# Two early expert tiles put among the last sequence's work, in products of 256 columns

## The chip, the cores and the metric

The kernel runs on one core of a Trainium2 chip. The time is device time of one execution in microseconds: the median of three runs before the change is 913.55 us (912.6 to 915.59). The engines are TensorE (PE; its weight loads are the row PEld), VectorE (DVE), ScalarE (ACT), GpSimd (POOL) and the DMA queue of SyncE (SP).

## What is computed

Two blocks on x of 16 sequences of 128 tokens and 256 columns, with a context of the same shape:

```
x = x + xattn0(layernorm(x), ctx)        # K K^T, lower triangle, times Q
x = x + ffn0(layernorm(x))               # RMS norm, 16-head causal attention of width 128 with rope,
                                         # then 2 of 8 experts per token: silu(t w1) * (t w3) w2, F 512
x = x + xattn1(layernorm(x), ctx)        # 16 heads of 64, softmax, output times tanh(gate)
x = x + ffn1(layernorm(x))               # 2 of 16 experts, F 256, and one shared expert
```

Each token goes to its two experts alone: the tokens are sorted into one run of rows per expert, and the experts work on tiles of 128 rows.

## The kernel before, in words

**Stages.** Sequence stage (b = 0 to 15): attention of both kinds, then for each sequence the router (`ra`, `cnt`, `rb`: places of its tokens in the experts' runs, L1740 to L1783), the cast of the places (`pi`) and a scatter of the token rows to memory (`sc`, two indirect DMAs, POOL). Expert stage 0: NT0 = 37 listed tiles beside the two early ones; the first 16 of the list are tiles of pairs with split weights (three products each, L829 to L831), the rest are single tiles (L1023). Then the cross attention with the gathers `ga` of the experts' results (L2328), expert stage 1, and the shared expert with the final sum.

**Early tiles.** AHEAD = 2 tiles are full whatever the last sequences hold. `a_route` (DVE, L1875 to L1910) lists them from the counts of COUNTED = 10 sequences; `a_xs` loads their rows (SP, L2398); then `a_xT` (two transposes, L1214), `a_xT_e` (ACT), `a_gate0/1`, `a_up0/1` (one product of 512 columns each, L1224, with the token rows as stationary operand; each is two records in the trace, as the type is f32), `a_silu` (ACT, L1480), `a_hm` (DVE, L1915), `a_hT` (L1234), `a_hT_e` (ACT, L1488), `a_down0/1` (two products of 256 columns each, L1243) and `a_y`. All take PSUM banks of the ring `s` (0 to 3), which the scores of the sequences use, so `a_xT` follows `s` of sequence 15.

**After sequence 15.** `route` (DVE, L1785 to L1873) makes the list of all expert tiles from the full counts and ends with two casts into TI (L1869, L1871). Behind it: `xs` loads the rows of a tile (SP, L2448), `wa`/`wv` (ACT L1395, DVE L2084) and `wdh`/`wdl` (ACT L1408, DVE L2053) split the expert's weights, `xT` transposes (L995), `xTh`/`xTl` (ACT L1417, DVE L2043) split the rows, and `gate` of tile 0 is the first expert product. `places` (DVE, L1917 to L1966, 27 instructions) lists where each token's results lie; the gathers `ga` wait for it and for the last store `ys` of results. `load_q` (L2500 on) loads the weights wq and wo of the cross attention (1 MB each), on SP, behind the last `down`.

**Order of the work.** No order is written by hand. `Plan.order` is a list scheduler: each phase has an engine, a booked duration in ns, what it follows, its banks and a due. Of all phases whose predecessors are laid out it takes the one with the smallest start + due, where due is that of the phase plus its LEAD from a table; it knows no table load of ACT and no clock. Each engine's instructions are issued in that order, so a phase that waits holds back those behind it on its engine. Sequence b has due 20 b; the early tiles have AHEAD_DUE = 400, and 20 more for the second.

**Names in the steps.** L932 and L923 scores, L1342 exp, L947 transposes of probabilities and L1349 their copies (the last two before PV are those of groups 2 and 0), L962 PV, L971 up-projection, L1731 residual, L1355 square, L979 and L980 count.

## Time and profile before

| | |
|---|---|
| median of 3 runs | 913.55 us |
| the profiled execution, its own time | 913.28 us |
| its span, first to last instruction | 911.5 us |
| mean granted TensorE clock | 0.985 |
| PE, DVE, ACT, POOL busy | 853.1, 709.4, 604.6, 287.2 us |

The stages by the trace: sequences to about 203 us, expert stage 0 from 214 to 403, cross attention from there to about 700, the rest to the end. Busy times are sums over the span; which engine sets the time differs by stage. The clock is given as a share of TensorE's full rate (1.00 is 2.4 GHz, 0.50 is 1.2 GHz; what lies between is a mean over a window).

### The profile page before, as it was taken

What the parts mean: (1) busy time and instruction counts of PE and PEld (TensorE: products, weight loads), DVE (VectorE), ACT (ScalarE), POOL (GpSimd) and SP (SyncE); (2) the same over time, 40 slices, a digit from 0 to 9 for tenths busy, and PEclk for the clock granted to TensorE, in tenths of its full rate; (3) what the DMA queues carried; (4) which work ended last, traced back from release to release, by engine and by line L of the source; (5) the groups of instructions that cost most, each with busy time, mean ns of one, the idle gap of its engine ahead of it and who ended that gap; (6) DMA issues with size and microseconds to landing.
All of it is one profiled execution on the core that took longest, in us unless ns stands there. A gap on an engine that the chain in (4) does not pass through costs nothing.

```text
span 911.5 us, 23338 instructions
## 1 busy us (share of the span) xinstructions
PE 853.1 (94%) x7726; PEld 762.7 (84%) x7726; DVE 709.4 (78%) x1990; ACT 604.6 (66%) x1718; POOL 287.2 (32%) x359
## 2 busy tenths in 40 slices
PE   5799989879999999996899999999999999999997
PEld 3677656538999999995898988998889889999996
DVE  4887898776887777786899888777688638888867
ACT  4388899956666676664777667778775327777740
POOL 3865577660000000005554542111023004444420
PEclk9999999979999999997999999999999999999999
DMA  8237700023312311031111121031044933333335
GB/s 316 74 117 269 320 24 26 31 87 112 116 59 70 141 47 59 25 109 50 34 42 36 43 81 67 19 100 36 2 185 191 366 76 92 103 94 100 101 113 200
DMA packets 43319, 94.23 MB, mean 103 GB/s; under 512 B 6112, under 2 KB 29536, under 8 KB 41664
## 3 DMA queue, kind: packets, MB, share of 16 engines
q1 hardware_dynamic: 36336, 73.93, 23.4%
q0 software_dynamic: 6864, 18.80, 6.0%
q8 instruction: 64, 1.05, 0.5%
q14 instruction: 55, 0.45, 0.2%
HBM read 63.53 MB, written 29.17 MB: 102 GB/s over the span
## 4 chain that ended last, share of the span: by engine, by line
PE 65%; DVE 8%; issue 2%; ACT 2%; DMA 1%; POOL 0%; ACTq 0%; SPq 0%; DVEq 0%; POOLq 0%
PE ps L1023 17%; PE ps L829 11%; PE ps L830 10%; PE ps L831 10%; PE ps L1116 3%; PE ps L1140 3%; PE ps L1126 3%; PE ps L1198 2%; DVE BIGR L2084 1%; PE ps L1224 1%; PE ps L995 1%; PE ps L996 1%; DMA ys_dram<-BIG 1%; DVE X L2119 1%; ACT BIGR L1395 1%
## 5 line engine op out<-in xcount | busy, mean ns | idle before, releaser
L829 PE MATMUL ps<-BIGR 128*128 128x256 f32 (+1 forms) x946 | 292.0, 309 | 7.5 <-DVE BIGR L2084 3.1
L831 PE MATMUL ps<-BIGR 128*128 128x256 f32 (+1 forms) x898 | 255.8, 285 | 0.0
L830 PE MATMUL ps<-BIGR 128*128 128x256 f32 (+1 forms) x722 | 211.7, 293 | 0.0
L829 PEld LDWEIGHTS ps<-BIGR 128*128 128x128 f32 x946 | 180.7, 191 | 14.3 <-issue 9.8
L1023 PE MATMUL ps<-BIG 128*128 128x128 f32 x1424 | 177.3, 275 | 0.0
L831 PEld LDWEIGHTS ps<-BIGR 128*128 128x128 f32 x898 | 171.1, 191 | 0.7
L1023 PEld LDWEIGHTS ps<-BIG 128*128 128x128 f32 x1424 | 168.1, 192 | 0.1
L830 PEld LDWEIGHTS ps<-BIGR 128*128 128x128 f32 x722 | 138.5, 192 | 1.8
L2328 POOL DMA_INDIRECT BIG<-ys_dram,YI x32 | 35.3, 1102 | 218.2 <-DMA ys_dram<-BIG 210.5
L1565 ACT ACTIVATE BIG<-ps,BIG 128x128 f32<-128x128 f32 x256 | 91.0, 383 | 13.2 <-DVE BIG L2164 12.9
L2313 POOL DMA_INDIRECT xs_dram<-TT,PI x64 | 65.5, 1023 | 86.2 <-ACT PI L1375 72.3
L2336 POOL DMA_INDIRECT yt_dram<-BIG,IX x47 | 55.3, 1177 | 115.4 <-DVE BIG L2077 112.8
L2053 DVE TENSOR_TENSOR BIGR<-BIG,BIGR 128x512 fp32r<-128x512 f32 (+1 forms) x76 | 67.9, 895 | 11.9 <-ACT BIGR L1408 9.2
L1342 ACT ACTIVATE BIG<-ps,BIG 128x128 f32<-128x128 f32 x256 | 71.7, 408 | 3.9 <-DVE BIG L1701 3.9
L830 PE MATMUL ps<-CTR,BIGR 128*128 128x256 f32 x224 | 63.2, 282 | 0.0
L2251 POOL TENSOR_TENSOR st<-st,CS 128x1 f32<-128x1 f32 (+1 forms) x48 | 30.4, 637 | 99.9 <-DVE st L1656 99.7
L2084 DVE TENSOR_TENSOR BIGR<-BIG,BIGR 128x1024 fp32r<-128x1024 f32 (+3 forms) x57 | 48.2, 864 | 15.8 <-ACT BIGR L1395 12.1
L1408 ACT CAST BIGR<-BIG 128x512 fp32r (+1 forms) x76 | 59.0, 777 | 0.0
L1565 ACT ACTIVATION_READ_ACCUMULATOR BIG<-ps,BIG 128x1 f32 x256 | 56.9, 222 | 0.0
L1573 ACT COPY BIG<-ps 128x512 f32<-128x512 f32 x64 | 38.6, 603 | 27.5 <-PE ps L1126 25.6
L2060 DVE TENSOR_TENSOR BIG<-ps,BIG 128x256 f32<-128x256 f32 (+1 forms) x84 | 45.2, 539 | 13.2 <-PE ps L1023 11.3
L1398 ACT COPY BIG<-BIG 128x512 f32 x47 | 29.1, 619 | 33.9 <-PE ps L1023 32.3
(304 smaller groups left out, 1873.4 us busy)
## 6 DMA issues: line engine op xcount, KB each, us to landing
BIG<-in_wgu SPq DMA_DIRECT2D x2, 6144.0 KB, 19.1
BIG<-in_wd SPq DMA_DIRECT2D x2, 4096.0 KB, 22.5
BIG<-xs_dram SPq DMA_DIRECT2D x47, 129.5 KB, 2.1
BIG<-xs_dram SPq DMA_DIRECT2D x37, 128.0 KB, 2.0
ys_dram<-BIG SPq DMA_DIRECT2D x37, 128.0 KB, 2.0
BIG<-in_wkv SPq DMA_DIRECT2D x2, 2048.0 KB, 9.5
kv_dram<-BIG SPq DMA_DIRECT2D x16, 256.0 KB, 2.1
BIG<-in_wgu SPq DMA_DIRECT2D x2, 2048.0 KB, 9.8
```

The lines of the kernel that those rows point to most:

```text
L829: pe.matmul(o, l[0], r[0], start=start, stop=False)
L830: pe.matmul(o, l[0], r[1], start=False, stop=False)
L831: return pe.matmul(o, l[1], r[0], start=False, stop=stop)
L1023: i = pe.matmul(o[:, c * 128:(c + 1) * 128], wt[:, at:at + 128], x[:, k * 128:(k + 1) * 128], start=k == 0, stop=k == 1)
L1342: i = act.activation(p_[g][:, at], ps("s", b, i=g)[:, at], ACT.Exp, bias=sm[:, 4 * g + n:4 * g + n + 1])
L1408: act.copy(D_[j % len(D_)][:, 0:n], WD[:, bass.ds(e * n, n)]).then_inc(S["down_hi"], 1)
L1565: i = act.activation(xp_[s % 4][:, at], ps("S", s // 2, i=s % 2)[:, at], ACT.Exp, bias=sm[:, 4 + n:5 + n], accum_out=sm[:, 8 + n:9 + n])
L2053: v.tensor_tensor(wd[:, n:2 * n], WD[:, bass.ds(e * n, n)], wd[:, 0:n].bitcast(F32), ALU.subtract).then_inc(S["down_lo"], 1)
L2060: v.tensor_tensor(h, ps("up", r_, j)[:, 0:F], h, ALU.mult).then_inc(*frees("up", r_, j))
L2084: return v.tensor_tensor(dst, src, hi.bitcast(F32), ALU.subtract)
L2313: pool.indirect_dma_start(XS if r else XS0, bass.IndirectOffsetOnAxis(ap=PI[:, b, k:k + 1], axis=0), TT[tile_of(r, b)][:, 0:ROW if r else ...
L2336: pool.indirect_dma_start(YT, bass.IndirectOffsetOnAxis(ap=IX[:, j:j + 1], axis=0), Y_[1][j % 3], None).then_inc(sem(f"results_placed{j % ...
```

## The change

- COUNTED is 9 instead of 10. The row loads of the early tiles wait for `ctx` of sequence 11 (COUNTED + 2) instead of 9.
- The first early tile has due 500 and takes banks of the ring `misc` (4 to 7), after `qkT` of sequence 15; the second has due 900 + 20 and the ring `s`, after `s` of sequence 15, as before. `a_route` has due 600.
- Gate, up and down of an early tile are four phases each of one product of 256 columns (booked 430 ns), where they were two of 860.
- `a_route` is four phases of 650 ns, `places` eight of 800 to 1250 ns, piece i after `wv` of tile 18 + i, due -2000 (it was one of 4400 after `wv` of tile 8, due 4000).
- `gate` of tile 0 follows `a_up3` of the second early tile, `gate` of tile 2 its `a_down3`.
- The table LEAD is replaced for the phases after the sequences; the leads of the sequence phases are the same, those of the early tiles are 0. Among the new ones: xTh0 533 to 1314, wa0 -172 to 643, xs0 -352 to -11820, load_q -19372 to -33060, ys0 -48558 to -13864, kwl -7379 to -26302, owl -17804 to -6563, gates_a -34755 to -23246.

```diff
-COUNTED = 10
-AHEAD_DUE = 400
+COUNTED = 9
+AHEAD_DUE = (500, 900)
+A_DUE = 600
...
-    p.add("DVE", 4400, ("places",), ("wv", 0, 8), due=4000)
+    for i, ns in enumerate((800, 950, 950, 950, 1250, 950, 950, 1250)):
+        p.add("DVE", ns, ("places", i), ("wv", 0, PAIRED + 2 + i), due=-2000)
...
-    p.add("DVE", 2200, ("a_route",), ("rb", 0, COUNTED - 1), due=AHEAD_DUE)
+    for i in range(4):
+        p.add("DVE", 650, ("a_route", i), ("rb", 0, COUNTED - 1), due=A_DUE)
...
-            p.add(engine, ns, (name, i), *after, banks=[("s", (q, i)) for q in banks], due=AHEAD_DUE + 20 * i, **kw)
-        add("SP", 700, "a_xs", ("a_route",), ("sc", 0, COUNTED - 1), ("ctx", COUNTED - 1), ("load_w0b",), late=2200)
-        add("PE", 220, "a_xT", ("a_xs", i), ("s", NB - 1), banks=["a_xT_e"])
-        add("PE", 860, "a_gate0", ("a_xT_e", i), ("a_reg", i), banks=["a_silu"])
-        add("PE", 860, "a_gate1", ("a_gate0", i))
-        add("PE", 860, "a_up0", ("a_gate1", i), banks=["a_hm"])
-        add("PE", 860, "a_up1", ("a_up0", i))
+            p.add(engine, ns, (name, i), *after, banks=[("s" if i else "misc", (q, i)) for q in banks], due=AHEAD_DUE[i] + 20 * i, **kw)
+        add("SP", 700, "a_xs", ("a_route", 3), ("sc", 0, COUNTED - 1), ("ctx", COUNTED + 2), ("load_w0b",), late=2200)
+        add("PE", 220, "a_xT", ("a_xs", i), ("s" if i else "qkT", NB - 1), banks=["a_xT_e"])
+        for which, bank in (("gate", "a_silu"), ("up", "a_hm")):
+            for x in range(4):
+                before = (f"a_{which}{x - 1}", i) if x else ("a_gate3", i) if which == "up" else ("a_xT_e", i)
+                add("PE", 430, f"a_{which}{x}", before, ("a_reg", i), banks=[] if x else [bank])
...
-            p.add("PE", 1440, ("gate", r, j), ("xTl", r, j0), ("wv", r, j), ("xTl", r, j0 + 1), banks=[("gate0", ("silu", r, j))], due=3 * j)
+            p.add("PE", 1440, ("gate", r, j), ("xTl", r, j0), ("wv", r, j), ("xTl", r, j0 + 1),
+                  *[("a_up3", AHEAD - 1) for _ in range(j == 0)], *[("a_down3", AHEAD - 1) for _ in range(j == 2)], banks=[("gate0", ("silu", r, j))], due=3 * j)
...
-                at = k * 2 * F0 + (F0 if which == "up" else 0)
-                m = pe.matmul(ps(*key)[:, :], AXT[i % 2][:, k * 128:k * 128 + 128],
-                              WGU[:, bass.ds(expert[i] * (4 * F0) + at, F0)], start=k == 0, stop=k == 1)
+                at = k * 2 * F0 + (F0 if which == "up" else 0) + half * D
+                m = pe.matmul(ps(*key)[:, half * D:half * D + D], AXT[i % 2][:, k * 128:k * 128 + 128],
+                              WGU[:, bass.ds(expert[i] * (4 * F0) + at, D)], start=k == 0, stop=k == 1)
```

## Rows read from the trace of the kernel before

**Rows 1.** Windows: us, PE, PEld, DVE, ACT, POOL busy (x instructions), PEclk, DMA share, GB/s

```profile
176.00:180.00 4.00, 3.21 (x47) 2.04 (x49) 2.75 (x13) 4.00 (x14) 1.19 (x2) 1.00 0.00 0
...
188.00:192.00 4.00, 2.36 (x36) 1.94 (x36) 1.40 (x11) 2.32 (x7) 2.64 (x4) 0.58 0.34 112
...
200.00:204.00 4.00, 4.00 (x8) 1.75 (x7) 3.51 (x23) 0.60 (x1) 1.96 (x3) 0.71 0.28 98
```

**Rows 2.** Chain of waits into the expert stage: start us, us, what

```profile
196.62 9.95 PE ps L1224 x16
...
213.03 1.05 DVE BIGR L2043 x4
...
214.32 0.35 PE ps L829
```

**Rows 3.** Timeline of DVE, last sequences: start us, us, engine, line, op, out<-in

```profile
184.43 0.15 DVE L1880 TENSOR_TENSOR sc<-CNT,CS 128x8 f32<-128x8 f32 x1
...
187.35 0.49 DVE L1731 SCALAR_TENSOR_TENSOR BIG<-BIG,st,ps 128x264 f32<-128x264 f32 x1
...
203.06 0.15 DVE L1871 CAST TI<-sc 128x1 int32<-128x1 f32 x1
```

**Rows 4.** Timeline of PE, last sequences and second early tile

```profile
180.24 1.08 PE L962 MATMUL ps<-BIG 128*32 128x128 f32 x32
...
184.10 0.67 PE L971 MATMUL ps<-small,BIG 128*128 128x264 f32 x2
...
189.84 1.94 PE L962 MATMUL ps<-BIG 128*32 128x128 f32 x32 [0.78 <-ACT BIG L1349]
...
193.53 1.22 PE L971 MATMUL ps<-small,BIG 128*128 128x264 f32 x2 [1.13 <-DVE BIG L1722]
...
202.97 3.60 PE L1224 MATMUL ps<-BIG,small 128*128 x8
```

**Rows 5.** Timeline of ACT over the same stretch

```profile
187.88 0.42 ACT L1355 ACTIVATE BIG<-BIG 128x256 f32<-128x256 f32 x1 [0.96 <-DVE BIG L1731]
...
198.57 1.28 ACT L1480 ACT_TABLE_LOAD   x1
200.43 0.60 ACT L1480 ACTIVATE CT<-ps 128x512 f32<-128x512 f32 x1 [0.57 <-PE ps L1224]
...
211.54 1.15 ACT L1417 ACTIVATE BIGR<-ps,small 128x128 fp32r<-128x128 f32 x4
```

**Rows 6.** Timeline of SP's queue: the first row loads of the expert stage

```profile
204.23 2.97 SPq L2448 DMA_DIRECT2D BIG<-xs_dram  x3
```

**Rows 7.** Page, DMA issues: out<-in, engine, xcount, KB each, us to landing

```profile
BIG<-xs_dram SPq DMA_DIRECT2D x37, 128.0 KB, 2.0
```

**Rows 8.** Timeline of PE in the expert stage: a pair tile and a single tile

```profile
250.55 0.33 PE L995 MATMUL ps<-CS,BIG 128*128 128x128 f32 x1
...
333.60 0.36 PE L829 MATMUL ps<-BIGR 128*128 128x256 f32 x1
```

**Rows 9.** Timeline of DVE in a single tile of the expert stage

```profile
331.08 0.69 DVE L2069 TENSOR_TENSOR BIGR<-BIG,BIGR 128x512 fp32r<-128x512 f32 x1 [0.56 <-ACT BIGR L1442]
332.15 1.23 DVE L2053 TENSOR_TENSOR BIGR<-BIG,BIGR 128x1024 fp32r<-128x1024 f32 x1 [0.38 <-ACT BIGR L1408]
```

**Rows 10.** Windows of the second boundary (columns as in the first group)

```profile
430.00:432.00 2.00, 2.00 (x15) 2.00 (x15) 1.96 (x3) 0.60 (x1) 2.00 (x1) 0.74 0.21 66
```

**Rows 11.** Timeline of PE at the second boundary

```profile
427.70 0.55 PE L829 MATMUL ps<-BIGR 128*128 128x256 f32 x1 [1.81 <-DVE BIGR L2084]
```

**Rows 12.** Timeline of DVE: places, first and last of its 27 instructions

```profile
403.84 0.16 DVE L1923 TENSOR_SCALAR BIG<-BIG 128x9 f32<-128x9 f32 x1
...
411.25 0.18 DVE L1966 CAST YI<-Y 128x32 int32<-128x32 f32 x1
```

**Rows 13.** Chain of waits at the second boundary

```profile
404.16 8.04 DMA ys_dram<-BIG
```

**Rows 14.** Windows of expert stage 0, 214 to 402: their sum

```profile
sum 188.00, PE 185.98 PEld 184.25 DVE 140.18 ACT 127.17 POOL 0.00; mean PE 26.57 PEld 26.32 DVE 20.03 ACT 18.17 POOL 0.00
```

More of the change, by code:

```diff
@@ L308, in ahead_phases @@
         add("PE", 450, "a_hT", ("a_hm", i), banks=["a_hT_e"])
-        add("ACT", 490, "a_hT_e", ("a_hT", i), ("a_down1", i - 2), *[("ctx", b) for b in (13,) if i % 2])
-        add("PE", 860, "a_down0", ("a_hT_e", i), banks=["a_y"])
-        add("PE", 860, "a_down1", ("a_down0", i))
-        add("ACT", 330, "a_y", ("a_down1", i))
+        add("ACT", 490, "a_hT_e", ("a_hT", i), ("a_down3", i - 2), *[("ctx", b) for b in (13,) if i % 2])
+        for x in range(4):
+            add("PE", 430, f"a_down{x}", (f"a_down{x - 1}", i) if x else ("a_hT_e", i), banks=[] if x else ["a_y"])
@@ L313, in ahead_phases @@
+        add("ACT", 330, "a_y", ("a_down3", i))
         add("SP", 60, "a_ys", ("a_y", i), late=2000)
@@ L372, in cross_phases @@
 def cross_phases(p):
-    p.add("SP", 100, ("load_kv",), ("down", 0, PAIRED - 1), ("a_down1", AHEAD - 1), due=0, late=12000)
+    p.add("SP", 100, ("load_kv",), ("down", 0, PAIRED - 1), ("a_down3", AHEAD - 1), due=0, late=12000)
     p.add("SP", 100, ("load_q",), ("down", 0, NT0 - 1), late=8000)
@@ L1215, in a_xT, with a_gate_up @@
                 pe.transpose(ps("a_xT", i)[:, 128:256], AXS[i][:, 128:256], ident).then_inc(*fills("a_xT", i))
-            def a_gate_up(i, which, k):
-                key = f"a_{which}0", i
-                if k == 0:
+            def a_gate_up(i, which, x):
+                key, half, k = (f"a_{which}0", i), x // 2, x % 2
+                if x == 0:
                     vacant(pe, *key)
@@ L1879, in a_route, with add_up @@
                 tiles = OHW[0].rearrange("p a n -> p (a n)")[:, 0:E * AHEAD].rearrange("p (n j) -> p n j", n=E)
-                v.tensor_tensor(nn, CNT[:, COUNTED, 0:E], ecap[0], ALU.subtract).then_inc(dv, next_step("dve"))
-                then()
-                v.tensor_tensor(tiles, nn.rearrange("p (n o) -> p n o", o=1).broadcast_to([128, E, AHEAD]),
-                                cst["cmp"][:, 1:1 + AHEAD].rearrange("p (o j) -> p o j", o=1).broadcast_to([128, E, AHEAD]),
-                                ALU.is_ge).then_inc(dv, next_step("dve"))
-                then()
-                v.tensor_reduce(steps[0][:, 8:16], tiles, AX, ALU.add).then_inc(dv, next_step("dve"))
-                for i in range(3):
-                    then()
+                inc, before = [steps[3][:, 8 - x:16 - x] for x in range(2)]
+                def add_up(i):
                     v.tensor_tensor(steps[i + 1][:, 8:16], steps[i][:, 8:16], steps[i][:, 8 - 2 ** i:16 - 2 ** i],
@@ L1891, in a_route @@
                 then()
-                v.tensor_scalar(steps[3][:, 8:16], steps[3][:, 8:16], float(AHEAD), None, ALU.min).then_inc(dv, next_step("dve"))
-                then()
-                inc, before = [steps[3][:, 8 - x:16 - x] for x in range(2)]
-                v.scalar_tensor_tensor(out=ahead_row, in0=before, scalar=-128.0, in1=ecap[0], op0=ALU.mult,
-                                       op1=ALU.add).then_inc(dv, next_step("dve"))
-                v.tensor_scalar(w1, inc, cst["j"], None, ALU.is_le).then_inc(dv, next_step("dve"))
@@ L1898, in a_route @@
-                then()
-                v.tensor_reduce(te, w1, AX, ALU.add).then_inc(dv, next_step("dve"))
-                v.scalar_tensor_tensor(out=behind, in0=inc, scalar=128.0, in1=ahead_row, op0=ALU.mult,
-                                       op1=ALU.add).then_inc(dv, next_step("dve"))
-                then()
-                v.scalar_tensor_tensor(out=w1, in0=iota[0][:, 0:E], scalar=te, in1=ahead_row, op0=ALU.is_equal,
-                                       op1=ALU.mult).then_inc(dv, next_step("dve"))
@@ L1915, in a_hm, with places @@
                 v.tensor_tensor(AH[i % 2], ps("a_up0", i)[:, :], AH[i % 2], ALU.mult).then_inc(*frees("a_up0", i))
-            def places():
+            def places(step_):
                 E, OHw, C = E0, OHW[0], RP[:, 128:137]
@@ L2400, in a_xs @@
                     sp.wait_ge(sem("ahead_listed"), 1)
-                    sp.wait_ge(*full("ctx", COUNTED - 1))
+                    sp.wait_ge(*full("ctx", COUNTED + 2))
                     sp.wait_ge(*done("ctxl", len(EARLY_KV) - 1))
```

156 lines of the change are left out of this document (90 added, 66 removed), and 27 rows, old and new, of the table LEAD.

## The prediction

> **What bounds the kernel now.** I read the windows of the trace first. TensorE is busy nearly all the time in the expert stage and after it, so a shift at the head of that stage lasts to the end unless a later stage takes it back. The stretch that is not full lies around the last two sequences: from 188 on TensorE is busy 2.36 of 4 us, its granted clock falls towards the lower level (0.58 for the window), and it is back at the upper one only within 200 to 204 (0.71) [rows 1]. The chain of waits says what this stretch is made of: after the count of sequence 15 stand 9.95 us of early-tile products (16 records, two early tiles); the end of the chain is the split of the expert's token rows on DVE and the first expert product at 214.32 [rows 2]. The list of expert tiles is ready at 203.06 + 0.15 = 203.2 [rows 3]. So 11.1 us pass between list and first product, though the list's followers need far less. That is the time the change can reach.
>
> **What the change moves, part by part.**
>
> *a_route.* It runs from 184.43 to 187.35 on DVE and holds back the residual of sequence 14 (L1731, 187.35) [rows 3], whose operand was there when L971 ended, at 184.77 [rows 4]. Behind it ACT sat idle 0.96 us and then ran the square, a scaling and the last two copies that PV of sequence 15 waits for [rows 5]. With COUNTED 9 and due 600 the list is made sequences earlier, in DVE's gaps, and no longer waits for the scatter of sequence 9. DVE gets 2.6 us back there, but ACT's idle time is all that lies on the path: **-0.96**. Behind the early list stand two SP loads; SP has nothing else in that stretch, and I cost them at nothing.
>
> *The first tile among sequence 15.* It may use a misc bank after qkT of 15, and its products come in 12 pieces. From the second tile's products (8 records, 3.60 us at the upper level, for gate and up) a 256-column piece is 0.45 us, and the four down pieces of a tile take 1.8 [rows 4]. TensorE has room for all of this (it is busy 2.36 of 4 us [rows 1]). What a piece costs is where it starts just before a step of sequence 15 becomes ready: between 0 and 0.45 each, before PV, the up-projection and the count. I take **+0.4** together (0 to 1.3).
>
> *Its Silu on ACT.* The table load before the first Silu takes 1.28 us at 198.57, now in a hole of ACT, and the Silu itself 0.60 [rows 5]. Among the sequences it either stands before the last copy of sequence 15 (1.28 + 0.60 = 1.9) or after it (nothing). The planner books 470 ns for it and no load, and its due of 500 against 300 plus small leads for the copies makes this a matter of tenths. I take **+0.9**, between 0 and 1.9. Between two Exps it would cost two loads, 2 x 1.28 + 0.6 = 3.2. The load is followed here by a wait for TensorE, so this row can't tell what comes behind a load. The Trainium skill, page "ScalarE: Activation LUTs", section "What ACT_TABLE_LOAD costs", adds a drain of about 1.38 us to every switch; by it the two places would cost 3.3 and 6.0 instead of 1.9 and 3.2, which speaks against this change. No row here shows that drain.
>
> *The clock.* PV takes 1.08 us at 180.24 and 1.94 at 189.84; the up-projection 0.67 at 184.10 and 1.22 at 193.53 [rows 4]. That is the fall of the clock after a thin stretch [rows 1]. With the first tile's products there, I expect the upper level through both: 0.86 + 0.55 = **-1.4** (0 if the clock falls all the same).
>
> So the list of tiles comes at 203.2 - 0.96 + 0.4 + 0.9 - 1.4 = 202.1.
>
> *From the list to the first product.* The early tiles no longer stand in front. SP issues the first of three row loads at 204.23, 1.0 after the list, and three take 2.97 us [rows 6]; a load lands in 2.0 [rows 7]. The second tile's rows are there 1.0 + 1.0 + 2.0 = 4.0 after the list; transposes 0.3 [rows 8], the tile's two activations 0.6 (half of 1.15 [rows 5]), its two DVE splits 0.5 (half of 1.05 [rows 2]) and some 0.6 of handing over give 6.0. The weight splits, 1.23 each [rows 9], run beside it. So 6.0 in place of 11.1: **-5.1**. Since gate (0, 0) only follows a_up3 of the second tile, whose products fit in the waits of sequence 15 and in the time of the route, this should hold. Its down products wait for DVE (behind the route) and for ACT (behind three casts), so their 1.8 us fall right before the first expert product, in time that is idle anyway.
>
> *What that gives back.* TensorE is now thin from about 4 us before the list to 5 after it. At the next such hole the row shows the price: the first product after it starts at 427.70 and TensorE is at the upper level from about 431, 3.3 us at half rate [rows 10, 11], a loss of 1.65. At the first boundary it took from 196.62 to about 202.4 (0.71 of the window 200 to 204 [rows 1]), 5.8 us, a loss of 2.9. I take **+2.0**, between 0 (the clock never falls) and 2.9. The Trainium skill, page "TensorE: Matmul & The Clock Gate", section "What's actually happening", calls the throttled state the default that only activity releases; by that the penalty is certain, and emptying TensorE before the experts is what this change does wrong.
>
> *places.* Its 27 instructions fill DVE from 403.84 to 411.43 [rows 12]. One would think they hold the first gather. They do not: the last result's store takes 8.04 us and lands at 412.20 [rows 13], as it is queued behind the load of the projection weights, which SP issues first and still will (load_q's lead is now -33060, ys0's -13864). So the gather waits 0.8 us longer than for places, and taking them away is worth **0** (down to -1 if the store lands sooner).
>
> In the single-tile part the pieces (0.75 to 1.2 us each) meet DVE's idle time: about 0.56 before L2069 and 0.38 before L2053 in each tile, and L2053 ends 0.2 before the product that needs it [rows 9, 8]. Six fit in 0.94 + 0.2; the two long ones stick out by 0.1. **+0.3** in all; were each put right before L2053, it would be 0.95 - 0.38 - 0.2 = 0.4 each, 3 in all.
>
> *The new leads.* The leads of the sequence phases are unchanged, so that stage keeps its order apart from what is put in. All later stages are laid out anew: 0, with a bound of 3 us either way.
>
> **Sum.** -0.96 + 0.4 + 0.9 - 1.4 - 5.1 + 2.0 + 0 + 0.3 = -3.9. The profiled execution took 913.28 us (span 911.5, 1.8 around it), 0.3 below the median shown. 913.3 - 3.9 = 909.4, against the median 909.7.
>
> **Rivals.**
>
> *The gain is eaten at the boundary (912.9).* The Silu stands between Exps or the penalty of the clock is whole, and pieces delay PV: 2.3 more for the one and 0.9 for the other, -3.9 + 3.2 = -0.7. For it: ACT is busy 4.00 of the 4 us before 180 [rows 1], so all work put there is on the path. Against it: the gate pieces can't be done before Exp of sequence 15 is nearly through.
>
> *More than forecast (905.8).* The clock stays up through the boundary (-2.0), the Silu falls behind the last copy (-0.9), and the second hole shrinks by 1 us as DVE is free: -3.9 - 3.9 = -7.8. Against it: both holes of the present kernel show the clock fall.
>
> *Slower (917.7).* In the pair tiles ACT casts and DVE splits both weights and rows, and the rows' transposes (L995 [rows 8]) stand in the middle of TensorE's products, so rows that come late stop all of it. The new leads put the row casts later (xTh0 533 to 1314). If one weight split (1.23 [rows 9]) gets ahead of the rows in each of the 8 pairs, TensorE waits 8 x 1.23 = 9.8 less what overlaps, some 8: 909.7 + 8 = 917.7. From 0.5 us a pair on the gain is gone; from 0.8 it is slower beyond the threshold. For it: TensorE is busy 185.98 of the 188 us of that stage [rows 14], so there is much to lose and little to win. Against it: the planner's durations for this stage are close to the trace.
>
> *It doesn't do what it says (913.6).* The planner puts the pieces behind the route all the same, since 500 to 920 is a high due: the early tiles stand in front as before, cut smaller.
>
> **Chances.** Forecast 0.48, eaten 0.22, more 0.12, slower 0.11, not done 0.07. A measurement tells this kernel from no change at about 0.3%, 2.7 us. The forecast case is spread by some 2 us about 909.7, so about four fifths of it is faster by more than that. Faster 0.54, same 0.32, slower 0.14. The range takes in the good case and most of the eaten one and the foot of the slow one: 904.5 to 915.5. The forecast case alone: 907 to 912.
>
> **What would show it.** Right: first L1224 record before 190 and granted clock 1.0 in 188 to 196; the early list's DVE instructions before 175; first L829 of the expert stage some 6 to 8 us after the list, at about 210, with a granted clock below 1 around it; DVE free after the last expert tile but the first gather still waiting for the store. Wrong: an ACT_TABLE_LOAD between Exps before 186; PV of sequence 15 later than 190.5; TensorE idle more than 4 us between 214 and 402; the first expert product after 213.

## The result, and the profile after

The changed kernel takes **918.05 us** (median of 18 runs, 914.87 to 922.46) against 913.81 of the kernel before beside it (18 runs): a ratio of **1.0048, 95% interval 1.0034 to 1.0062**. It is 4.2 us slower; forecast was 909.7 with a range to 915.5. The profiled execution spans 920.7 us and took 922.46, the longest of the 18, so its stages have to be read with two sums taken out of them, falls of the clock that other executions of the same steps don't have (below).

In the code of after, a line of TensorE's or ScalarE's functions has a number 4 or 5 higher and one of VectorE's functions behind the route 13 or 14 higher: L829 is L833, L1224 is L1229, L1408 is L1412, L1234 is L1239, L1915 is L1928, L2043 is L2057, L2053 is L2067, L2060 is L2074, L2069 is L2083, L2084 is L2098, L2036 is L2050.

The windows of after that answer to [rows 1]; columns as there:

```profile
176.00:180.00 4.00, 3.00 (x41) 1.97 (x30) 3.51 (x13) 3.98 (x16) 0.90 (x1) 1.00 0.02 4
188.00:192.00 4.00, 2.87 (x12) 1.95 (x12) 2.57 (x11) 3.85 (x13) 3.49 (x5) 0.50 0.30 102
200.00:204.00 4.00, 3.61 (x17) 2.85 (x15) 3.69 (x18) 2.74 (x6) 3.21 (x4) 1.00 0.18 65
208.00:212.00 4.00, 3.97 (x14) 3.13 (x13) 2.78 (x4) 3.15 (x5) 0.00 (x0) 0.50 0.36 102
```

TensorE is busy longer in 188 to 192 than before (2.87 for 2.36 us), in part because the clock is at the lower level in all of it. It is back for all of 200 to 204 (0.71 in [rows 1], 1.00 here), and is low again in 208 to 212, where before had early products. The timeline of TensorE from its first early product to the first expert product (the list of tiles is ready at 206.11 + 0.15 in this execution):

```profile
191.54 1.22 PE L1229 MATMUL ps<-BIG,btg 128*128 x2 [0.27 <-ACT btg L1476]
...
200.00 3.62 PE L1229 MATMUL ps<-BIG,small 128*128 x16
207.67 1.94 PE L1239 MATMUL ps<-CS,CT 128*128 128x128 f32 x8 [4.05 <-DVE CT L1928]
209.63 2.92 PE L1247 MATMUL ps<-BIG,CT 128*128 x6
212.35 0.42 PE L999 MATMUL ps<-CS,BIG 128*128 128x128 f32 x1
...
215.47 0.33 PE L999 MATMUL ps<-CS,BIG 128*128 128x128 f32 x1 [0.77 <-DVE BIGR L2057]
...
216.18 0.35 PE L833 MATMUL ps<-BIGR 128*128 128x256 f32 x1 [0.27 <-DVE BIGR L2057]
```

The early tiles' gate and up products (L1229) did go between those of sequence 15 and in the time of the route, but their second half did not: transposes (L1239) and down products (L1247) wait 4.05 us for VectorE, which multiplies hidden and gate (L1928) only behind the route, and then stand at half clock ahead of the first row transpose. List to first product is 9.9 us, 11.1 before [rows 2, 3], 6.0 forecast.

TensorE's waits from 214 to 410, that is in the expert stage: engine, line, waited for, us in total, times, longest.

```profile
PE ps L833 <- DVE BIGR L2067: 1.9, 1, 1.9
PE ps L833 <- DVE BIGR L2057: 1.5, 2, 1.3
PE ps L999 <- DVE BIGR L2057: 0.8, 1, 0.8
PE ps L833 <- issue: 0.2, 1, 0.2
```

Those are 4.4 us, and 1.9 of them are one wait before the last tile's down products. They don't explain the whole stage, and in the second expert stage hardly a wait of TensorE is shown. There the **cadence** must be read: the time from one row transpose (L999, before L995) to the next, which is one tile.

| tiles | before | after |
|---|---|---|
| first stage, single tiles 22 to 36 | 5.21 to 5.24 us | 5.22 and 5.5 in turn, 5.36 on average |
| second stage, 47 tiles | 2.72 us | 2.78 us |

And the same milestones of seven kernels' profiled executions, in us after the up-projection of sequence 8, where the change has touched nothing yet:

| | before | after | places_only | early_only | s1_leads | s0_spliced | spliced_tail |
|---|---|---|---|---|---|---|---|
| sequence 8's up-projection, in the trace | 135.75 | 137.87 | 136.06 | 135.35 | 137.94 | 135.67 | 137.54 |
| sequence 15's up-projection | 57.78 | 59.31 | 57.80 | 56.99 | 56.99 | 56.92 | 57.09 |
| list of tiles | 67.31 | 68.24 | 67.35 | 66.00 | 66.00 | 65.92 | 66.09 |
| first expert product | 78.57 | 78.31 | 78.10 | 73.92 | 75.52 | 75.18 | 75.74 |
| its 96th record | 91.07 | 92.39 | 92.11 | 91.28 | 89.60 | 89.25 | 89.80 |
| its 480th record | 141.51 | 142.24 | 142.49 | 141.70 | 139.44 | 139.13 | 139.65 |
| last result of the first stage | 267.76 | 272.00 | 268.73 | 267.94 | 269.11 | 266.84 | 266.68 |
| list of the second stage | 575.61 | 579.05 | 577.96 | 576.72 | 575.74 | 572.26 | 572.21 |
| first row transpose of the second stage | 610.05 | 612.63 | 612.41 | 611.14 | 609.26 | 605.83 | 605.78 |
| last result of the second stage | 742.28 | 749.33 | 744.63 | 743.37 | 740.51 | 737.09 | 737.04 |

The two sums to take out are in the first two rows. In 5 of the 16 profiled executions of this study TensorE's granted clock fell at 26 us and was back at 33, for 2 us, with the same instructions in the same order as in the others. And in sequence 15 it fell in some and not in others: with the early pieces the up-projection of 15 stood at 56.9 to 57.1 in 7 of 12 executions (two of these have a granted clock of about 0.8 in 184 to 192, the others 1.00) and at 58.2 to 59.3 in 5. After's execution has both. With s1_leads' figures up to the 480th record (the same order of steps up to there, clock up in sequence 15) and after's steps behind it, the change reads: boundary 139.44 - 141.51 = **-2.1**; rest of the first stage 129.76 - 126.25 = **+3.5**; second boundary and second sequence stage 307.05 - 307.85 = -0.8; from the second list to its first transpose 33.58 - 34.44 = -0.9; the second stage's tiles 136.70 - 132.23 = **+4.5**. The sum is +4.2, the measured 4.2, but that it meets it to the tenth is luck, for two of its steps are soft.

The boundary compares one execution of s1_leads, with the clock up in sequence 15, with one of before, with the clock at 0.50 there from 192 to 200. The clock of that stretch is not the same in every execution. The 480th record stands at 139.1 to 142.2, 140.0 on average, in the eight kernels whose steps are after's up to there (after, s1_leads, s0_order, s0_places, s0_tail, s0_spliced, tail_order, spliced_tail), and at 140.5 to 142.5, 141.5 on average, in the four without early pieces. So the boundary won about 1.4 us on average and not 2.1. And the step of -0.8 is 305.4 to 308.2 us in the kernels with the new order there and 306.3 to 309.2 in those with the old one. The steps of +3.5, -0.9 and +4.5 are firm: the kernels that share after's order in one of these stretches take the same time there within 0.2 us.

### The profile page after: what moved, and what is told of

It is laid out like the page before. It is cut to its first block, busy times and chain, and to the rows that moved or that the text cites. A ratio compares the mean times of both kernels' runs of the same rounds, so it can differ in the third digit from the quotient of the medians.

```text
span 920.7 us, 23381 instructions
## 1 busy us (share of the span) xinstructions
PE 863.2 (94%) x7742; PEld 773.4 (84%) x7742; DVE 705.5 (77%) x1990; ACT 612.4 (67%) x1720; POOL 278.7 (30%) x359
## 4 chain that ended last, share of the span: by engine, by line
PE 69%; DVE 5%; ACT 3%; issue 2%; DMA 1%; POOL 0%; SPq 0%; DVEq 0%; ACTq 0%; POOLq 0%
PE ps L1027 17%; PE ps L833 12%; PE ps L834 11%; PE ps L835 11%; PE ps L1120 4%; PE ps L1144 3%; PE ps L1130 3%; PE ps L1202 2%; ACT BIG L1569 1%; PE ps L999 1%; PE ps L1000 1%; DMA ys_dram<-BIG 1%; DVE BIGR L2098 1%; PE ps L989 1%; PE ps L1247 1%
## 5 line engine op out<-in xcount | busy, mean ns | idle before, releaser
L833 PE MATMUL ps<-BIGR 128*128 128x256 f32 (+1 forms) x946 | 293.1, 310 | 9.4 <-issue 2.2
L833 PEld LDWEIGHTS ps<-BIGR 128*128 128x128 f32 x946 | 180.8, 191 | 19.3 <-issue 13.8
L1027 PE MATMUL ps<-BIG 128*128 128x128 f32 x1424 | 181.9, 276 | 0.8 <-issue 0.7
L1569 ACT ACTIVATE BIG<-ps,BIG 128x128 f32<-128x128 f32 x256 | 91.1, 381 | 14.0 <-DVE BIG L2178 13.6
L2342 POOL DMA_INDIRECT BIG<-ys_dram,YI x32 | 32.6, 1018 | 221.8 <-DMA ys_dram<-BIG 214.2
L2350 POOL DMA_INDIRECT yt_dram<-BIG,IX x47 | 47.2, 1003 | 127.1 <-DVE BIG L2091 124.3
L2067 DVE TENSOR_TENSOR BIGR<-BIG,BIGR 128x512 fp32r<-128x512 f32 (+1 forms) x76 | 70.1, 923 | 8.8 <-ACT BIGR L1412 7.3
L1412 ACT CAST BIGR<-BIG 128x512 fp32r (+1 forms) x76 | 59.0, 776 | 7.4 <-DVE TI L1875 3.6
L2098 DVE TENSOR_TENSOR BIGR<-BIG,BIGR 128x1024 fp32r<-128x1024 f32 (+3 forms) x57 | 48.6, 865 | 18.6 <-ACT BIGR L1523 7.9
L1434 ACT ACTIVATE BIG<-ps 128x256 f32<-128x256 f32 (+1 forms) x84 | 40.4, 481 | 26.2 <-DVE BIGR L2083 20.6
L1428 ACT COPY BIG<-ps 128x256 f32<-128x256 f32 x68 | 25.2, 371 | 41.5 <-PE ps L1027 30.4
```

The lines of the kernel that those rows point to most:

```text
L833: pe.matmul(o, l[0], r[0], start=start, stop=False)
L1027: i = pe.matmul(o[:, c * 128:(c + 1) * 128], wt[:, at:at + 128], x[:, k * 128:(k + 1) * 128], start=k == 0, stop=k == 1)
L1412: act.copy(D_[j % len(D_)][:, 0:n], WD[:, bass.ds(e * n, n)]).then_inc(S["down_hi"], 1)
L1434: act.activation(H_[r][j % 2], ps("gate", r, j)[:, 0:F_[r]], ACT.Silu).then_inc(*frees("gate", r, j))
L1569: i = act.activation(xp_[s % 4][:, at], ps("S", s // 2, i=s % 2)[:, at], ACT.Exp, bias=sm[:, 4 + n:5 + n], accum_out=sm[:, 8 + n:9 + n])
L2067: v.tensor_tensor(wd[:, n:2 * n], WD[:, bass.ds(e * n, n)], wd[:, 0:n].bitcast(F32), ALU.subtract).then_inc(S["down_lo"], 1)
```

## The experiments

Theory A: the new leads gave the two expert stages orders that cost 8 us, twice what the boundary and the parts behind it won. Its rivals: B, the pieces of places lengthen the single tiles; C, the early tiles themselves cost it. Each time is a median of 6 to 12 runs, with 11 to 32 runs of the kernel before beside them on the same chip. Times of different groups come from different chips, so where two variants are compared the ratios count.

| kernel | us | before beside it | ratio, 95% interval |
|---|---|---|---|
| places_only | 914.42 | 913.93 | 1.0006 (0.9989 to 1.0024) |
| early_only | 913.54 | 913.93 | 0.9997 (0.9981 to 1.0013) |
| s0_order | 919.62 | 913.93 | 1.0050 (1.0028 to 1.0073) |
| s1_leads | 914.45 | 913.93 | 1.0002 (0.9984 to 1.0019) |
| s0_places | 916.49 | 913.18 | 1.0039 (1.0025 to 1.0053) |
| s0_tail | 915.50 | 913.18 | 1.0019 (1.0005 to 1.0033) |
| hm_first | 917.00 | 913.18 | 1.0033 (1.0017 to 1.0050) |
| all_three | 917.17 | 913.18 | 1.0034 (1.0020 to 1.0048) |
| old_leads | 913.45 | 912.90 | 1.0007 (0.9986 to 1.0027) |
| s0_spliced | 912.34 | 912.90 | 0.9991 (0.9974 to 1.0009) |
| before_s1_new | 917.65 | 913.11 | 1.0058 (1.0037 to 1.0079) |
| before_s0_new | 924.23 | 913.11 | 1.0123 (1.0104 to 1.0142) |
| tail_order | 916.58 | 912.90 | 1.0042 (1.0028 to 1.0057) |
| spliced_tail | 911.31 | 912.90 | 0.9973 (0.9960 to 0.9987) |

**Each part of the change alone, with the old leads.** places_only is before with these lines (and `places` written in eight steps, as in the change):

```diff
-    p.add("DVE", 4400, ("places",), ("wv", 0, 8), due=4000)
+    for i, ns in enumerate((800, 950, 950, 950, 1250, 950, 950, 1250)):
+        p.add("DVE", ns, ("places", i), ("wv", 0, PAIRED + 2 + i), due=-2000)
```

> The kernel before with one part of the change: the places in eight pieces among the single tiles (their phases behind the tiles PAIRED + 2 to PAIRED + 9), nothing else; all leads are those of before, only that of places is 0 as in the changed kernel. Theory A (the time was lost by the order of VectorE's and ScalarE's steps in the expert stages, which the new leads set): the pieces fill idle time of VectorE (0.94 us in each single tile of before), the single tiles keep their 5.22 us from row transpose to row transpose, and the kernel is 0 to 3 us faster than before, as the first gather no longer waits for 27 instructions (913.8 to 910.8 by before's median). Theory B (the pieces slow the single tiles): the single tiles take 5.34 or more where pieces stand, and the kernel is 1 to 3 us slower than before.

No difference. Two single tiles of its VectorE timeline begin like this (start, us, engine, line; L1926 and L1929 are a piece of places, L2038 splits the next weights, L2071 the hidden rows, L2055 the down weights):

```profile
299.35 0.75 DVE L2038 TENSOR_SCALAR BIG<-BIG,small 128x1024 f32 x1
300.02 0.42 DVE L1926 TENSOR_TENSOR BIG<-OH,BIG 128x256 f32<-128x256 bf16 x1
300.47 0.42 DVE L1929 TENSOR_REDUCE BIG<-BIG 128x32 f32<-128x256 f32 x1
301.01 0.69 DVE L2071 TENSOR_TENSOR BIGR<-BIG,BIGR 128x512 fp32r<-128x512 f32 x1
302.08 1.23 DVE L2055 TENSOR_TENSOR BIGR<-BIG,BIGR 128x1024 fp32r<-128x1024 f32 x1 [0.38 <-ACT BIGR L1409]
...
304.56 0.75 DVE L2038 TENSOR_SCALAR BIG<-BIG,small 128x1024 f32 x1
```

The piece fills the 0.56 us that [rows 9] show ahead of the hidden split, and the tiles stay at 5.21 to 5.24. Rival B falls in its plain form. The 0 to 3 us that theory A hoped for at the second boundary did not come either.

early_only is before with the list from nine sequences, the pieces of 256 columns, their banks and dues, and old leads.

> The kernel before with the other part of the change: the list from nine sequences, the early tiles in products of 256 columns between the last sequence's; the leads of all other phases and the single step for places are those of before. Theory A (orders in the expert stages cost the time, the boundary is neutral): first expert product 0 to 1 us earlier than before, counted from the end of sequence 15's count; single tiles again at 5.22 us with VectorE in the order product with the gate, row weights, result, two splits; the expert stages' steady tiles 5.22 and 2.72 us, total within 1.5 us of before (912.3 to 915.3). Theory C (the early tiles themselves cost it: three table loads on ScalarE, pieces at half clock, a longer thin stretch for TensorE): first expert product 1 us or more later than before and the total 2 to 4 us above before.

No difference in the end, but a large one in between: the first expert product comes 4.65 us earlier, and by the 96th record 0.2 later than before's. Part of the early work had only moved behind the first product, and behind it TensorE stands idle for 1.16 us, for nothing that the profile names. Its timeline:

```profile
216.26 2.32 PE L1246 MATMUL ps<-BIG,CT 128*128 x10
219.74 0.36 PE L832 MATMUL ps<-BIGR 128*128 128x256 f32 x1 [1.16 <-issue]
```

So the time is neither gained nor, as Theory C had it, lost by 2 to 4 us.

old_leads has both parts and old leads (in the diff of the change, all but the table; the early phases' and places' leads are 0).

> Both parts of the change (early tiles and places in pieces) with all leads as the kernel before had them (0 for the early phases and for places). Each part alone ran as fast as before (ratios 1.0006 and 0.9997). Theory A (the new leads are what cost 4 us): steady tiles at 5.22 and 2.72 us, total 913 to 914.5. Rival G (the parts together need the new leads, without them it is slower still, by the planner 2.6 us more than with them): 918 or more.

913.45: with before's leads the whole change costs nothing and brings nothing. **So the 4 us hang on the new leads**, and rival G falls. It has the tiles of 5.22 and 2.72 us. The new leads have a good side too: the boundary's gain hangs on them as well. With the early tiles and before's leads the 480th record comes at 141.7 (early_only, clock up in sequence 15) and 143.1 (old_leads), no earlier than before's 141.5. So the new leads cost 8.0 us in the two expert stages and bring back 1.7 between them and about 2 at the boundary; what is left, by the two ratios, is 0.41%.

**The second expert stage.** s1_leads is after with the 23 leads of that stage (names that end in 1) as before had them.

> The changed kernel with the leads of the second expert stage alone as before had them. Theory A: the 47 tiles go from 2.78 us back to 2.72 and the start of the stage is as before: 46 x 0.06 = 2.8 us and up to 1 more, 914.3 to 915.3 against the changed kernel's 918.05. Rival D (the 2.78 us are no matter of order but of the stage's state, such as the clock or VectorE's own duration for the down split, 0.75 against 0.69): cadence stays 2.78, 918.

918.05 to 914.45 (ratio 1.0048 to 1.0002, intervals apart), cadence 2.72. What the order does there is seen in ScalarE's waits over 26 tiles (790 to 860), first before:

```profile
ACT BIG L1398 <- PE ps L1023: 18.9, 25, 1.2
ACT BIG L1398 <- issue: 0.5, 1, 0.5
```

and after:

```profile
ACT BIG L1434 <- DVE BIGR L2083: 11.8, 25, 0.8
ACT BIG L1402 <- issue: 5.8, 25, 0.2
```

Before, ScalarE waits for TensorE in each tile: TensorE sets the pace. In after no wait of ScalarE or VectorE for TensorE is listed in this stretch at all; Silu (L1434) waits for VectorE's hidden split (L2083), as the new order puts that split, and the result ahead of it, one tile later and behind the next hidden product:

```
before  DVE: hm j   wv j+2  y j-1  ix j+3  hl j    wdl j+1
after   DVE: hm j   wv j+2  ix j+3  y j-2  hl j-1  wdl j
```

That ScalarE and VectorE now drive each other in a loop of 2.78 us is the likely reading, but only one half of it is in the list: ScalarE's wait for VectorE. VectorE's own wait, 0.35 us before each weight split (L2050), is put down to issue, so what it waits for is not shown. TensorE has no gap in a tile that is printed as a wait; two of its records, the first down product and the second product of the group behind the down products, start some 0.03 us later after the one ahead of them than in before. The mirror of it, before with the new order in this stage alone (15 leads):

> The kernel before with nothing of the change but the leads of the second expert stage's tile phases (all but hl1), so that its plan takes there the order of the changed kernel: result and hidden split one tile later, gate two tiles and not one ahead of down. Early tiles, places and all other stages as before. Theory A (order alone makes the loop of 2.78 us): 47 tiles at 2.78 in place of 2.72, the stage from its first row transpose to its last result 136.5 in place of 132.2 us, total 3 to 4.5 us over before. Rival D (the loop needs something else of the changed kernel): 2.72, no difference.

917.65, and its ScalarE waits are after's:

```profile
ACT BIG L1430 <- DVE BIGR L2069: 11.9, 25, 0.8
ACT BIG L1398 <- issue: 5.5, 24, 0.2
```

The stage took 135.90 against 132.23 us (136.5 expected). The order alone is the cause, in either kernel, and rival D falls.

**The single tiles of the first stage.** After's plan has `wv` of tile j + 3 ahead of `hm` of tile j + 1. Both wait for the same up product, so the hidden product starts 0.67 us later, and with it all that ends in the down split (L2067). The down products start 0.14 us behind the end of that split in after, in the tiles of 5.22 and of 5.5 us alike; in before they start 0.2 behind it. VectorE in one tile of before, hidden product and down split:

```profile
354.78 0.69 DVE L2060 TENSOR_TENSOR BIG<-ps,BIG 128x512 f32<-128x512 f32 x1 [0.51 <-PE ps L1023]
...
358.27 1.23 DVE L2053 TENSOR_TENSOR BIGR<-BIG,BIGR 128x1024 fp32r<-128x1024 f32 x1 [0.38 <-ACT BIGR L1408]
```

and in one of after, with the down product behind it:

```profile
354.47 0.75 DVE L2050 TENSOR_SCALAR BIG<-BIG,small 128x1024 f32 x1 [1.16 <-PE ps L1027]
355.14 0.68 DVE L2074 TENSOR_TENSOR BIG<-ps,BIG 128x512 f32<-128x512 f32 x1
355.74 0.42 DVE L2091 COPY BIG<-ps 128x256 f32<-128x256 f32 x1
356.51 0.69 DVE L2083 TENSOR_TENSOR BIGR<-BIG,BIGR 128x512 fp32r<-128x512 f32 x1 [0.35 <-ACT BIGR L1446]
357.58 1.23 DVE L2067 TENSOR_TENSOR BIGR<-BIG,BIGR 128x1024 fp32r<-128x1024 f32 x1 [0.38 <-ACT BIGR L1412]
...
358.95 0.36 PE L833 MATMUL ps<-BIGR 128*128 128x256 f32 x1
```

Two runs changed VectorE's order there and, on ScalarE, only put the split of the hidden rows ahead of that of the down weights. s0_order, behind the planner:

```diff
+    new = [k for j in range(17, 35) for k in [("hm", 0, j), ("wv", 0, j + 2), *extra[j], ("y", 0, j - 1), ("hl", 0, j), ("wdl", 0, j)]
+           if k in part]
```

> The changed kernel with one order changed: in the single tiles 17 to 34 of the first expert stage VectorE takes the steps of a tile as before did (hidden times gate of tile j, then weights of tile j + 2, places piece, result of j - 1, the two splits), in place of the weights of tile j + 3 ahead of the hidden product of tile j + 1; ScalarE splits the hidden rows ahead of the down weights throughout. Theory A: the single tiles go from 5.34 us on average to 5.22 although the places pieces stay where they are, 18 x 0.13 = 2.3 us less: 915.7 against the changed kernel's 918.05. Theory B (the pieces slow the tiles, not the order): tiles with a piece stay at 5.34 or more, at most 1 us gained.

> The changed kernel with one order changed: single tiles 17 to 34 of the first expert stage in the order that the run with places alone had (VectorE: hidden times gate of tile j, weights of j + 2, places piece, the two splits, then the result of j - 1 while there are pieces; result first after them). The run with the order of s0_order put result and piece ahead of the splits and its first tiles took 6.62, 6.03 and 5.83 us. Theory A: all single tiles at 5.22 us, 18 tiles from 5.34 on average to 5.22, about 2.0 us less than the changed kernel: 916. Rival B (what holds the tiles is ScalarE's or TensorE's order, which stays the changed kernel's): tiles stay at 5.34 or more where the pieces stand.

Both miss. s0_order was no faster than after (919.62; ratio 1.0050 against 1.0048), and s0_places (916.49) by 0.1% at best (1.0039, intervals overlap): its first stage from the 480th record on took 130.2 us, no less than after's 129.8. Behind the last piece the tiles are at 5.22 in both, as expected, but among the pieces four tiles take 5.5 to 6.6 in the one, and in the other one takes 6.6 and five 5.3 to 5.6. VectorE's order was changed while TensorE's and most of ScalarE's stayed; that this is why the tiles with pieces got no shorter was argued, and the next run bears it out. s0_spliced takes the order of all four engines for tiles 18 on from a second plan, made with before's leads there, on top of s1_leads:

```diff
+    for engine, first in (("PE", "K"), ("DVE", "cl"), ("ACT", "ch"), ("SP", "load_kv"), ("SP", "load_kv")):
+        ks, rank = orders[engine], {k: i for i, k in enumerate(again[engine])}
+        cut = [k[0] for k in ks].index(first)
+        ks[:cut] = sorted(ks[:cut], key=rank.get)
...
```

> s1_leads (914.45 us) with the first expert stage's single tiles from 18 on in the order that before's leads give, on all engines at once (TensorE, ScalarE, VectorE and SyncE; not VectorE's alone as in s0_places), the rest of the plan unchanged. Theory A: tiles from the 20th on at 5.22 us with the pieces of places between them, the stage from its 480th product to the last result 126.3 to 127.5 us in place of 129.7, total 911 to 912.5. Rival B: the pieces need the new order, and tiles with a piece stay at 5.3 to 5.6 us: 914 or more.

912.34, ratio 0.9991 against 1.0002 of s1_leads; the intervals overlap, so the gain is read from the tiles. From the 23rd row transpose on all tiles are at 5.21 to 5.24, those with pieces too, and that part of the stage takes 127.7 us in place of 129.7. VectorE's hidden product (L2088 here) leads again:

```profile
358.34 0.69 DVE L2088 TENSOR_TENSOR BIG<-ps,BIG 128x512 f32<-128x512 f32 x1 [0.50 <-PE ps L1041]
359.10 0.76 DVE L2064 TENSOR_SCALAR BIG<-BIG,small 128x1024 f32 x1
359.77 0.42 DVE L2105 COPY BIG<-ps 128x256 f32<-128x256 f32 x1
```

The mirror, before with the new order from tile 18 on and no pieces there:

> The kernel before with nothing of the change but the order of the first expert stage's single tiles from 18 on, on all engines as the changed kernel's leads give it (weights of tile j + 3 ahead of the hidden product of tile j + 1 on VectorE), without any piece of places there. Theory A: tiles at 5.22 and 5.5 us in turn, 5.35 on average, 2 to 3.5 us over before. Rival B (the pieces of places are needed to lengthen the tiles): 5.22 us, no difference.

The tiles are as theory A says, 5.22 and 5.5 in turn and 5.37 on average over the last 14, without any piece. The total (924.23, far above the 2 to 3.5 us expected) is no measure of it: at the seam of the two plans four tiles took 10.28, 7.09, 7.00 and 13.36 us, where no tile of before took more than 6.7.

**The last tile.** TensorE waits 1.87 us in after before the last down products, 0.53 in before.

> s1_leads (914.45 us) with the single tiles' order of s0_places, and in the last tile VectorE's splits of the key and value weights behind, no longer ahead of, the hidden product of tile 36, with ScalarE's split of the hidden rows of tile 36 ahead of the down weights'. Theory A: 2.0 us from the tiles, and TensorE's wait of 1.86 us before the last down products down to about the 0.53 that the kernel before had, 1.3 us: 914.45 - 3.3 = 911.1. Rival B: what is gained at the end of the stage is lost at the second boundary, where the splits moved back are needed next: 912.5 to 914.

It gave 915.5, no better than s1_leads and as neither theory had it, and TensorE's wait grew to 2.3 us. The wrong step had been moved: the result of tile 35 still stood ahead of the hidden product of tile 36, and VectorE waited 2.0 us there for the down products of 35. tail_order is after with before's seven steps:

```diff
+    last = [("hm", 0, 36), ("kwl", 0), ("vwl", 0), ("hl", 0, 36), ("btg",), ("wdl", 0, 36), ("y", 0, 35)]
+    d[at:at + 7] = last
```

> The changed kernel with VectorE's seven steps after the down split of tile 35 in the order of the kernel before: hidden product of tile 36 first, then the splits of key and value weights, the hidden split, the bias row, the down split, and the result of tile 35 last; ScalarE splits the hidden rows of tile 36 ahead of its down weights. Theory A: the wait before the last down products falls from 1.87 us to about 0.5, and 1.3 us of it last to the end, 918.05 to 916.7. Rival B: the second boundary takes it back, as it waits for the splits moved behind: no change in time, 918.

The wait is back at 0.5, in TensorE's waits from 385 to 412:

```profile
PE ps L843 <- issue: 0.5, 1, 0.5
```

The time is 916.58, 1.5 less than after's; as ratios 1.0042 and 1.0048, whose intervals overlap, so the gain at the end is likely and not settled by this run alone. Counted from the 480th record the last result came 0.8 us earlier (128.98 for 129.76) and the second list 1.35.

**The boundary.** In s1_leads the clock stays up through sequence 15, and this is the stretch from list to first product (SPq is the DMA queue of SyncE):

```profile
203.94 0.15 DVE L1875 CAST TI<-sc 128x1 int32<-128x1 f32 x1
...
204.67 1.28 DVE L1928 TENSOR_TENSOR CT<-ps,CT 128x512 f32<-128x512 f32 x2
...
205.11 2.97 SPq L2462 DMA_DIRECT2D BIG<-xs_dram  x3
205.50 1.94 PE L1239 MATMUL ps<-CS,CT 128*128 128x128 f32 x8 [3.97 <-DVE CT L1928]
...
207.47 2.92 PE L1247 MATMUL ps<-BIG,CT 128*128 x6
...
210.19 0.38 PE L999 MATMUL ps<-CS,BIG 128*128 128x128 f32 x1
```

By an estimate the first rows land at 205.11 + about 1.0 of issue + 2.0 (the page's issue to landing) = 208.1, and TensorE comes to their transpose at 210.19. hm_first has the first early tile's hidden product ahead of the route:

```diff
 NUDGE = {
+    ("a_hm", 0): -1000,
 }
```

> s1_leads (914.45 us) with one due time: the first early tile's hidden product on VectorE 1 us earlier in rank, so that the plan puts it between two steps of sequence 15, and its transposes and down products go in front of the second tile's last products and into the route's time. Theory E (the early tiles' second half stands between list and first expert product: eight transposes and six down pieces, 4.9 us at the lower clock, of which xs rows ready at about 207.3 had to wait until 210.2): list 0.4 to 0.7 later, first expert product 1.5 to 2.5 us earlier counted from the end of sequence 8, total 912.5 to 913.5. Rival F (the work is only moved, every product in front of the list delays the list by as much): first expert product where it was, total 914 to 915.

The first product did come 1.6 us sooner after the list (7.9 us), and yet the time is 917.0, 2.5 above s1_leads. Counted from the up-projection of sequence 15 the list was 0.85 later, and the clock:

```profile
204.00:208.00 4.00, 1.07 (x6) 0.70 (x6) 2.13 (x10) 2.55 (x3) 0.00 (x0) 0.80 0.17 45
208.00:212.00 4.00, 2.21 (x8) 1.09 (x6) 4.00 (x7) 2.02 (x6) 0.00 (x0) 0.50 0.39 118
212.00:216.00 4.00, 3.98 (x19) 3.70 (x18) 0.69 (x3) 1.36 (x4) 0.00 (x0) 0.50 0.39 106
```

against s1_leads:

```profile
204.00:208.00 4.00, 2.47 (x9) 2.07 (x10) 2.81 (x8) 2.42 (x3) 0.00 (x0) 0.50 0.30 98
208.00:212.00 4.00, 3.76 (x14) 2.63 (x12) 2.66 (x3) 2.44 (x7) 0.00 (x0) 0.70 0.25 76
212.00:216.00 4.00, 2.98 (x23) 2.77 (x24) 1.74 (x6) 2.02 (x8) 0.00 (x0) 1.00 0.42 128
```

In s1_leads the early work runs at the lower level, and the clock is up again some 3 us before the first expert product at 213.46. In hm_first TensorE has less to do ahead of it, and the clock is still low for 4 us behind the first product, so that 96 records take 16.0 us in place of 14.1. So theory E's 1.6 us came, half of it went as F had it (the list 0.85 later), and the clock, which neither theory had, took more than the rest. Of the 2.5 us hm_first shows 1.1 (from the up-projection of 15 to the 96th record). all_three, whose front is the same and whose up-projection of 15 stood within 0.2 us of s1_leads', shows 1.5 (96th record at 91.1 for 89.6). Where the rest went stays open.

**Together.**

> All edits together: changed kernel, second stage's leads of before, single tiles' order, last tile's order, first early tile's hidden product earlier. If the shares add: 914.45 - 3.3 - 1.5 = 909.6, 0.5 per cent below the kernel before. If they are eaten at the second boundary: 912 or more, no better than before.

917.17: with hm_first and the wrong tail in it, no better than either. Its tiles with pieces were those of s0_places. The version without these two and with the right tail:

> s0_spliced (912.34 us) with the same seven steps of VectorE in the order of the kernel before. If the share of the tail adds: 911.0, 0.2 to 0.3 per cent below the kernel before. If the second boundary takes it back: 912.3.

**911.31, ratio 0.9973 (0.9960 to 0.9987)**: 0.27% below the kernel before and 0.75% below the changed one. It is the change with its two parts as they are, and the old orders in the single tiles, at the end of the first stage and in the second expert stage.

## Why the prediction was wrong

The step that failed is *the new leads*: "All later stages are laid out anew: 0, with a bound of 3 us either way." They cost 8.0 us by the profile's steps (+3.5 in the first expert stage, +4.5 in the second), outside that bound, and won 1.7 in what lies between, so +6.3 stands where 0 was forecast for the later stages. The second term that failed is *from the list to the first product* with what it gives back, below: by the profile's steps the boundary and all ahead of it brought 2.1 where the terms sum to 4.2. These two, 6.3 and 2.1, less 0.3 for the pieces of places, are the 8.1 us between the forecast of -3.9 and +4.2. The second expert stage was not read at all in the prediction, although its leads were changed with the rest (hm1 from -16585 to -1230, hh1 from 156 to 1269): a loop of 2.78 in place of 2.72 us over 46 tiles is 2.8, and its start and its last tiles cost the rest. That [rows 14] show TensorE busy 185.98 of 188 us was read as "little to win"; what it meant was that any order which lets another loop be longer than TensorE's costs at once.

Step by step:

- *a_route, pieces, Silu, clock: the list at 202.1.* In early_only it was at 201.35 and in s1_leads at 203.94, which counted from sequence 8 is 1.3 us earlier than before in both; the terms summed to -1.1. The sum was right where the clock stayed up, in part by luck: the 0.9 for Silu was not paid, so the others brought less than their terms, and before_s1_new, whose front is before's, has its list 0.8 us earlier than before's execution with no change there at all. So of the 1.3 us only some 0.5 is more than executions of one plan differ by. What the pieces did show is the clock: it is back at 0.86 or more in 196 to 200 in all 12 executions that have them and at 0.50 in the four without; in after's profiled execution it fell in sequence 15, and the list came 0.9 late. The early list itself was not made "before 175": its four pieces lay between 157.76 and 182.57 in s1_leads, and the first early product came at 191.46.
- *Silu, +0.9.* It cost nothing visible. ScalarE loads its table three times, not once, all in its holes:

```profile
193.41 1.28 ACT L1484 ACT_TABLE_LOAD   x1
194.70 0.60 ACT L1484 ACTIVATE CT<-ps 128x512 f32<-128x512 f32 x1
...
196.70 1.28 ACT L1365 ACT_TABLE_LOAD   x1
...
199.45 1.28 ACT L1484 ACT_TABLE_LOAD   x1
200.75 0.60 ACT L1484 ACTIVATE CT<-ps 128x512 f32<-128x512 f32 x1
```

  The Silu starts 0.01 to 0.02 us behind its load, both times. The Trainium skill, "ScalarE: Activation LUTs", section "What ACT_TABLE_LOAD costs", puts a drain of 1.38 us on every switch; the traces of this kernel show none behind the load, nor ahead of it (0.02 us from the end of the instruction ahead). The trace of before could have told so: of its loads, that at 695.44 has no wait behind it, and the next activation starts at 696.74.

```profile
695.44 1.28 ACT L1605 ACT_TABLE_LOAD   x1
```
- *List to first product, 11.1 to 6.0.* This mechanism was right in kind and its size wrong: 9.5 with the clock up. The sum let the down products alone stay behind, "in time that is idle anyway". Six records of them, and eight transposes that it did not count, took 4.9 us at the lower clock in front of the first row transpose, and six more records came behind the first expert product, inside the 96. So -5.1 was -1.7, and +1.6 came back at once: the 96 records took 14.1 us for 12.5.
- *Clock given back, +2.0.* TensorE is at half rate from about 203.6 to 210.4 in s1_leads, as the windows show, but mostly over early products and not the expert stage's. hm_first shows the price where they are gone. The Trainium skill, "TensorE: Matmul & The Clock Gate", section "What's actually happening", speaks of the throttled state as the default; the granted clock of 0.50 in 204 to 208 of s1_leads, behind 4 us without a product, agrees. But in 188 to 192 of the same execution TensorE is busy 2.05 of 4 us and the clock is 1.00, where before's had fallen to 0.58 with 2.36 busy, so a thin stretch does not bring the fall each time.
- *places off the second boundary, 0, and in the single tiles +0.3.* Both right to within 0.3: the last store still lands 7.50 us after its issue at 411.46 (8.04 in [rows 13]), and the pieces cost nothing with the old order.
- *Second boundary.* 0 was forecast; the new leads won 0.9 from list to first transpose, and 0.8 ahead of it, which the executions do not settle.

Of the rivals, the slower one named the right place, the expert stage, and the wrong mechanism: late row casts in the pair tiles. The pair tiles from the 96th to the 480th record took 49.9 us against 50.4 before, no loss at all. The price it gave (917.7) agrees with the result by accident. Of "it doesn't do what it says" half came true: the early tiles' second half stayed behind the route. And the boundary alone, -2.1 or, on average, -1.4, lies between the forecast's -4.2 and the -0.7 of the rival that had the gain eaten there.

## What to carry to other kernels

Where a planner's table is refitted for an edit, the stages that the edit does not touch are part of the change: lay out both plans, compare the order of steps within one steady tile on each engine, and cost each stage's tile times its count. A kernel whose plan books the same time can have a longer loop on the chip; see who waits for the busiest engine before and after. In this case nobody waited for it any longer, and the order alone had made the tile longer. And work taken from in front of a stage is worth less than its duration when the stage's first products then run at the lower clock, as in hm_first, or when it only moves behind the point that was being watched, as in early_only.

## What the runs showed that was not expected

- VectorE's down split of 128x512 takes 692 ns on average in the second stage of before (26 records) and 749 ns in after, 746 in before_s1_new: its duration differs with the order alone, by about the 0.06 us that the tile grew. Whether the longer split makes the longer tile or both come of the order is open.
- The granted clock fell at 26 us in 5 of 16 executions with the same instructions in the same order up to there, for 2 us of time (hm_first had a shorter fall there). All of them are kernels with new leads, 10 of the 16; whether that is chance is open. In sequence 15 the early pieces' kernels lost 1.2 to 2.3 us in 5 of 12 executions. Together the two spread single executions by some 4 us, as much as the change cost.
- The 0.06 us by which each tile of the second stage grew, 2.8 us over 46 tiles, is in no list of TensorE's waits; only the cadence shows it.
